# A decoder layer on one core: operand stacks filled from their half tiles, semaphores of each stage, and the order in which feed-forward weights are turned

## The chip, the cores and the metric

The kernel runs on one core of one Trainium2 chip. Its engines work side by side and wait for each other through semaphores: TensorE (PE; its weight loads are PEld), VectorE (DVE), ScalarE (ACT), GpSimd (POOL) and SyncE (SP), which here only issues DMAs. The metric is the device time of one launch in microseconds (us). Time before is the median of three runs.

## The reference

One layer of a transformer decoder on 8 sequences of 256 tokens, width 512, everything in float32 precision (the kernel reaches it by splitting each operand in a high and a low part in fp32r and multiplying high by high, high by low and low by high).

```python
x = x + self_attention(layernorm(x))       # 16 heads, decay states, gated
x = x + cross_attention(layernorm(x), ctx, mask)
x = x + feed_forward(layernorm(x))         # w1, w2, w3 first quantized to NF4 and back

# cross-attention, per sequence b: x[b] and ctx[b] are taken as [channel 256][t 512]
q = Wq @ x[b] + bq;  k = Wk @ ctx[b] + bk;  v = Wv @ ctx[b] + bv
dot = einsum('hdt,hds->hts', q, k) / 4     # 16 heads of 16
dot = mask_t * mask_s * dot - (1 - mask_t * mask_s) * 1e6
out = einsum('hts,hds->hdt', softmax(dot) * mask, v)

# feed-forward, d_ff = 1408
h = silu(x @ w1.T) * (x @ w2.T);  y = h @ w3.T
```

## The kernel before

The three parts are three stages of one program, one after the other. Each has a block of its own, in which every engine has its own list of instructions, and ends with `clear`, a further block in which GpSimd clears the stage's semaphores: all engines meet before and behind it. Memory (`big`, of which the tiles q_big in the trace are parts) is handed from one stage to the next.

**Self-attention** (0 to 1460 us in the trace) is not touched but for its end. There it also computes the query and key projection of cross-attention's sequence 0, in `xhi` and `xlo` (a_wqk_h and a_wqk_l in the trace), and SP prepares the first operand stacks Q0 and K0 from them.

**Cross-attention** goes over 8 sequences ("batches") b, each of 4 quads (4 heads), each quad of 4 steps q of four score tiles; G = 4 * (quad in the batch) + q runs from 0 to 15. For sequence b+1, `take_projection` (VectorE, `full`), `high` (ScalarE, `hi`) and `low` (GpSimd or VectorE, `lo`) make the halves of the projections while b's scores are computed; the buffer x_lo is also `full`. Three pairs of stacks Q[b % 3] and K[b % 3] hold the operands of a score product: for each half e of 8 heads, three segments of 16 partitions (high, high, low for Q; high, low, high for K), then rows of the mask, and in Q one row (53) with the row maxima. A segment is filled by `fill_part`, 256 KB. TensorE computes the scores of a quad twice, first over 53 partitions (x_pm, line 1720) for VectorE to find each row's maximum; the maxima are turned by TensorE (line 1725, one product for each quad), sent out to DRAM and back into row 53 (`rows`, two DMAs behind a wait), and then the product over 54 partitions (x_pd, line 1734) feeds the exponential on ScalarE. The products with V (x_pa, line 1748) follow.

SP's order in cross-attention is written out: at every step of G it waits for `dot_ready`, then issues what is due. The list `FILLS` says which segments of which stack go out at which G, `SECOND` says it for sequence 1. `put_part` (and `put` in self-attention) writes a half tile to DRAM (512 KB), and `fill_part` reads it back in the stack's layout; 4 puts and 12 fills for each sequence. `rows(t + 1)` stands at q = 1, `spread` at q = 0, `store` at q = 3 of every second quad.

**Feed-forward** first turns the three weights (22 + 11 tiles of 4 transposes each, TensorE line 2010, bf16) into `w1`, `w2`, `w3`, of which ScalarE and VectorE copy every second tile from a bank of pa; the loop `TILES` sets the order, w1, w2, w3. Then the first 512 tokens are turned, and `step` runs four times over 512 tokens: products with w1 and w2 (f_pa, f_pb, line 2028), silu, high and low, products with w3 (f_po, line 2042).

## Time and profile before

| | |
|---|---|
| median of 3 runs | 2402.73 us (2401.16 to 2409.71) |
| the profiled execution | 2406.03 us, span 2404.3 us |
| mean granted TensorE clock | 0.943 of full speed |
| PE busy | 2189.0 us (91%) |
| PEld, DVE | 1535.4 (64%), 1602.9 us (67%) |
| ACT, POOL | 791.9 (33%), 761.2 us (32%) |
| PE waits for x_K<-parts_scratch before x_pm | 23.9 us |

The profiled execution is one more run, its time 1.7 us longer than its span (from first to last instruction); it stands 3.3 us above the median. Busy shares are means over three stages with different limits. A row of a timeline or of a group names line, engine, operation and out<-in; what ended the idle time before an instruction stands in brackets behind it.

### The profile page before, as it was taken

Reading aid. Unit: us, or ns where it says so; the run is one execution under the profiler, and the core shown is the slowest. Engines: PE = TensorE matmul, PEld = TensorE weight load, DVE = VectorE, ACT = ScalarE, POOL = GpSimd, SP = SyncE. Lnnn points to the kernel's source line nnn. Section 1 sums busy time; section 2 is a strip of 40 time slices with the busy share of each in tenths; the row PEclk is TensorE's granted clock in tenths of the full one; section 3 lists DMA queues with packets and bytes.
Section 4 is the critical chain, followed back from the end, with each engine's and each line's share of the span. In section 5 each row is a group of like instructions: output and inputs, shape, how many; then the busy total and the mean of one; then the engine's idle time right before and its main releaser. Section 6 shows DMA issues by size and latency. Waiting matters only on the chain. (4 is left out here: it accounts for less than half of the span.)

```text
span 2404.3 us, 35495 instructions
## 1 busy us (share of the span) xinstructions
PE 2189.0 (91%) x11638; PEld 1535.4 (64%) x11638; DVE 1602.9 (67%) x2880; ACT 791.9 (33%) x1836; POOL 761.2 (32%) x532
## 2 busy tenths in 40 slices
PE   6899999999998999999999994988888887589998
PEld 4677778777776787778878772333332332167777
DVE  6668788788875568878878853687676876342221
ACT  1313323322332322332232320355444555432221
POOL 3334434533533433433443332112211220112122
PEclk9999999999999999999999996798898998669999
DMA  5211101101102201101110025765556643201100
GB/s 192 85 39 51 37 26 50 56 7 56 50 33 71 97 2 57 50 19 44 50 56 7 28 47 143 121 125 117 117 94 121 133 106 79 87 35 53 53 35 18
DMA packets 58838, 159.05 MB, mean 66 GB/s; under 512 B 9615, under 2 KB 24407, under 8 KB 52215
## 3 DMA queue, kind: packets, MB, share of 16 engines
q1 hardware_dynamic: 57142, 155.82, 24.9%
q10 hardware_dynamic: 1600, 2.02, 0.2%
q8 instruction: 52, 0.85, 0.2%
q14 instruction: 44, 0.35, 0.1%
HBM read 115.09 MB, written 34.33 MB: 62 GB/s over the span
## 5 line engine op out<-in xcount | busy, mean ns | idle before, releaser
L1627 DVE TENSOR_REDUCE x_mx<-x_pm 128x1 f32<-128x512 f32 x512 | 315.9, 679 | 108.4 <-PE x_pm L1720 107.2
L1490 ACT ACTIVATE x_E<-x_pd 128x512 f32<-128x512 f32 x512 | 265.4, 603 | 216.5 <-PE x_pd L1734 215.8
L1084 PE MATMUL a_pj<-q_big,a_wqk_h 128*128 128x512 f32 x1024 | 290.0, 405 | 1.0 <-POOL a_wqk_l L634 1.0
L1100 PE MATMUL a_pj<-a_wvg_h,q_big 128*128 128x512 f32 x1024 | 286.1, 406 | 1.1 <-DVE a_rm L790 1.0
L1100 PEld LDWEIGHTS a_pj<-a_wvg_h,q_big 128*128 128x128 f32 x1024 | 185.3, 188 | 51.8 <-DVE a_rm L790 2.4
L1084 PEld LDWEIGHTS a_pj<-q_big,a_wqk_h 128*128 128x128 f32 x1024 | 182.9, 188 | 40.4 <-POOL a_wqk_l L634 1.5
L790 DVE TENSOR_TENSOR a_rm<-a_pj,a_rope 128x1024 f32<-128x1024 f32 x128 | 155.7, 1217 | 79.4 <-PE a_pj L1084 78.1
L526 ACT ACTIVATE a_v<-a_pj 128x256 f32<-128x256 f32 x128 | 49.1, 384 | 416.0 <-PE a_pj L1100 416.0
L666 POOL TENSOR_TENSOR a_ogl<-a_ogf,a_ogh 128x512 fp32r<-128x512 f32 x64 | 81.7, 1298 | 286.6 <-ACT a_ogf L562 286.6
L1748 PE MATMUL x_pa<-x_E,x_vx 128*32 128x512 f32 x1024 | 149.8, 660 | 0.0
L862 DVE TENSOR_TENSOR a_acc<-a_po,a_acc 128x512 f32<-128x512 f32 x128 | 85.9, 687 | 93.7 <-PE a_po L1213 93.7
L1720 PE MATMUL x_pm<-x_K,x_Q 53*128 53x512 f32 x320 | 112.6, 484 | 32.1 <-DMA x_K<-parts_scratch 23.9
L1100 PE MATMUL a_pj<-a_wvg_l,q_big 128*128 128x512 f32 x512 | 140.7, 397 | 0.0
L1084 PE MATMUL a_pj<-q_big,a_wqk_l 128*128 128x512 f32 x512 | 140.1, 395 | 0.0
L1734 PE MATMUL x_pd<-x_Q,x_K 54*128 54x512 f32 x320 | 109.3, 494 | 21.5 <-ACT x_E L1490 17.3
L1734 PEld LDWEIGHTS x_pd<-x_Q,x_K 54*128 54x128 f32 x320 | 45.5, 196 | 127.8 <-ACT x_E L1490 72.2
L1857 POOL TENSOR_TENSOR f_hl<-f_hf,f_hh 128x512 fp32r<-128x512 f32 x44 | 56.6, 1285 | 213.2 <-ACT f_hh L1898 213.2
L796 DVE RECIPROCAL a_enz<-a_mid 128x512 f32<-128x512 f32 x32 | 107.2, 3351 | 16.7 <-PE a_mid L1068 16.7
L1100 PEld LDWEIGHTS a_pj<-a_wvg_l,q_big 128*128 128x128 f32 x512 | 96.7, 189 | 23.5
L553 ACT ACTIVATE a_sq<-a_po 128x128 bf16<-128x128 f32 x256 | 67.2, 277 | 133.9 <-PE a_po L1125 133.0
L1084 PEld LDWEIGHTS a_pj<-q_big,a_wqk_l 128*128 128x128 f32 x512 | 96.0, 187 | 23.4
L1213 PE MATMUL a_po<-a_wo_h,a_ogh 128*128 128x512 f32 x256 | 106.1, 414 | 3.0 <-POOL a_ogl L666 3.0
(215 smaller groups left out, 4573.5 us busy)
## 6 DMA issues: line engine op xcount, KB each, us to landing
a_qk_raw<-in_wqk SPq DMA_DIRECT2D x16, 1024.0 KB, 5.5
a_vg_raw<-in_wvg SPq DMA_DIRECT2D x16, 1024.0 KB, 4.9
q_big<-parts_scratch SPq DMA_DIRECT2D x36, 256.0 KB
...
```

What stands on the lines that cost most here:

```text
L666: nc.gpsimd.tensor_tensor(ogl[:, h, :], ogf[:, h, :], ogh[:, h, :].bitcast(F32), ALU.subtract).then_inc(ogl_done, 1)
L790: nc.vector.tensor_tensor(turned, pb, table, ALU.mult).then_inc(roped_m, 1)
L796: nc.vector.reciprocal(enz[:, p], ps[:, 0, :].rearrange("p (t m) -> p t m", t=4)).then_inc(enz_done, 1)
L862: nc.vector.tensor_tensor(a, po[:, tt % 2, :], a, ALU.add).then_inc(added, 1)
L1084: last = mm(pj[:, j % 2, :], wa[:, c, j * P:(j + 1) * P], xa[:, c, p * UT:(p + 1) * UT], start=k == 0, stop=k == 11)
L1100: last = mm(pj[:, tt % 2, :], xa[:, c, t0:t0 + P], wa[:, c, :], start=k == 0, stop=k == 11)
L1213: last = mm(po[:, tt % 2, :], oa[:, h, tt * P:(tt + 1) * P], wa[:, h, :], start=k == 0, stop=k == 5)
L1490: nc.scalar.activation(E[:, n % ESLOTS, :], pd[:, n % 3, :], ACT.Exp, scale=XD ** -0.5).then_inc(exp_done, 1)
L1627: nc.vector.reduce_max(mx[:, u % 2, at:at + 1], pm[:, k % 3, :], AX_X).then_inc(pm_done, 1)
L1720: mm(pm[:, k % 3, :], Q[b % 3][z, hp, q * P:(q + 1) * P], K[b % 3][z, hp, :], start=True, stop=True).then_inc(pm_ready, 1)
L1734: mm(pd[:, n % 3, :], K[b % 3][z, hp, q * P:(q + 1) * P], Q[b % 3][z, hp, :], start=True, stop=True).then_inc(dot_ready, 1)
L1748: last = mm(pa[32 * i:32 * i + 32, 0, :], vx[:, b % 3, q, head(t, i)].rearrange("p d k -> p (d k)"), E[:, k % ESLOTS, :], start=q == 0, st ...
```

## The change

Three things are changed together.

1. `fill_part` takes a segment of a stack straight from the half tiles in SBUF (64 partitions of 4 KB to 16 partitions of 16 KB). `put`, `put_part`, the DRAM tensor `parts` and their semaphores are gone. With them `FILLS` changes: in the second half of each batch all 12 fills for b+2 are issued (before: most in the first half of b+1). Since a fill now reads `hi` and `lo`, VectorE waits in `take_projection(b, 0)` for all fills of the stack b-1.
2. The semaphores of a stage come from a scope of their own, and are cleared by GpSimd inside the next stage: self-attention's behind `values(1, 1)` in cross-attention, cross-attention's behind `prepare(0)` in feed-forward. The two blocks between the stages are gone.
3. In feed-forward w1 and w2 are turned first, in pairs, w1 in pa and w2 in pb, the copies being divided anew (VectorE the first 7 tiles of w2, ScalarE the others), with the turns of x between the last pairs. The 11 tiles of w3 are turned inside the first `step`, one behind each pair of products, in the banks of po, and copied by ScalarE (`take_w3`). x comes in two halves, and `ident` on ScalarE's queue.

```diff
-def clear(nc, semaphores):
-
-    with nc.Block() as block:
-        @block.gpsimd
-        def _(pool):
-            for sem in semaphores:
-                pool.sem_clear(sem)
+def clear(pool, semaphores):
+
+    for sem in semaphores:
+        pool.sem_clear(sem)
...
-def fill_part(dma, tile, w, e, seg, split_dram, sem):
+def fill_part(dma, tile, w, e, seg, halves, sem):
 
     z = slice(64 * e + 16 * seg, 64 * e + 16 * seg + 16)
-    dma(tile[z].bitcast(F32),
-        split_dram[ORDERS[w][seg], w, 64 * e:64 * e + 64].rearrange("(r j) o t -> r (j o) t", j=4)).then_inc(sem, 16)
+    dma(tile[z].bitcast(F32), halves[ORDERS[w][seg]][64 * e:64 * e + 64, 2 * w:2 * w + 2].bitcast(F32)).then_inc(sem, 16)
...
+            fill(Q0, 0)
             store(1, 0)
-            put(1, ck_out)
-            sp.wait_ge(ck_out, 32)
-            for e in range(2):
-                for seg in range(3):
-                    fill_part(sp.dma_start, K0, 1, e, seg, split_dram, stack_0)
+            fill(K0, 1)
             store(1, 1)
             sp.wait_ge(stack_0, 16 * 16)
             sp.wait_ge(out_done, 16 * HALVES * HTILES)
...
-    clear(nc, s.used)
...
-        FILLS = [(0, (2,)), (0, (3,)), (0, (4, 5)), (1, (0, 1)), (1, (2,)), (1, (3,)), (1, (4, 5))] + 9 * [(0, ())]
+        FILLS = 8 * [(0, ())] + [(0, (0, 1)), (0, (2, 3)), (0, (4, 5)), (1, (0, 1)), (1, ()), (1, (4, 5)), (1, (2,)), (1, (3,))]
...
-            def put_part(b, w, part):
-                n = slice(2 * w, 2 * w + 2)
-                if b > 1 and not w and not part:
-                    sp.wait_ge(stack_in[(b - 1) % 3], stacked(b - 1))
-                sp.wait_ge((hi_done, lo_done)[part], 4 * (b - 1) + 2 * w + 2)
-                sp.dma_start(split_dram[part, w], (hi, lo)[part][:, n].bitcast(F32)).then_inc((q_split, k_split)[w], 16)
-
...
             def stack(b, w, pieces):
                 for k in pieces:
-                    if k == 0:
-                        sp.wait_ge((q_split, k_split)[w], 32 * b)
-                    fill_part(sp.dma_start, (Q, K)[w][b % 3], w, k % 2, k // 2, split_dram, stack_in[b % 3])
+                    part = ORDERS[w][k // 2]
+                    sp.wait_ge((hi_done, lo_done)[part], 4 * (b - 1) + 2 * w + 2)
+                    fill_part(sp.dma_start, (Q, K)[w][b % 3], w, k % 2, k // 2, (hi, lo), stack_in[b % 3])
 
...
             rows(0)
-            for w in range(2):
-                for part in range(2):
-                    put_part(1, w, part)
...
-                        stack(b + 1, *(FILLS if b else SECOND)[G])
+                    if not b:
+                        stack(1, *SECOND[G])
                     if t == 0 and q == 2:
                         load_c(2)
                     if b + 2 < B:
                         if G in (6, 7):
                             mask_rows(b + 2, G - 6)
-                        if 9 <= G < 13:
-                            put_part(b + 2, (G - 9) // 2, (G - 9) % 2)
+                        stack(b + 2, *FILLS[G])
                         if G == 12 and b + 3 < B:
                             load_x(b + 3)
                         if G == 13 and b + 3 < B:
                             load_c(b + 3)
-                        if G >= 14:
-                            stack(b + 2, 0, (G - 14,))
...
             values(1, 0)
             values(1, 1)
+            clear(pool, spent)
             for b in range(B):
...
-                    after(dve, (q_split, k_split)[j // 2], 32 * (b - 1))
+                    if j == 0 and b > 1:
+                        dve.wait_ge(stack_in[(b - 1) % 3], stacked(b - 1))
                     nc.vector.scalar_tensor_tensor(full[:, j, :], src[:, 0, :], bqk_t[:, j:j + 1], mb[:, b % 4],
...
-    clear(nc, s.used)
-
-
-def feed_forward(nc, x2_in, raw, big, ident_in, identb_in, out):
...
-        TILES = []
-        for i, w in enumerate((w1, w2)):
-            for r in range(FT):
-                TILES.append((i, [(slice(r * D + c * P, r * D + (c + 1) * P)) for c in range(C)],
-                              w[:, :, r * P:(r + 1) * P]))
-        for r in range(FT):
-            TILES.append((2, [slice(q * FF + r, q * FF + r + (P - 1) * FT + 1, FT) for q in range(4)],
-                          w3[:, r, :].rearrange("p (d q) -> p q d", q=4)))
+        BY_DVE = 7
+        MIXED = FT - 3
+
+        def turned(i, r):
+
+            return pa[:, r % 2, 0:256].bitcast(BF16) if i == 0 else pb[:, r % 2, 0:256].bitcast(BF16)
+
...
 
             prepare(0)
+            clear(pool, spent)
             step(0, True)
...
-            for t, (i, cols, dst) in enumerate(TILES):
-                if t % 2 == 0:
-                    act.wait_ge(w_ready, t + 1)
-                    src = pa[:, t % 2, 0:256].bitcast(BF16)
-                    nc.scalar.activation(dst, src.rearrange("p (q n) -> p q n", q=4), ACT.Copy).then_inc(taken_act, 1)
+            act.dma_start(ident[:], ident_in).then_inc(ident_done, 16)
+
+            def take(i, r):
+                act.wait_ge(w12_ready, 2 * r + i + 1)
+                nc.scalar.activation((w1, w2)[i][:, :, r * P:(r + 1) * P], spread(turned(i, r)), ACT.Copy).then_inc(taken_act, 1)
+
+            def take_w3(r):
+                act.wait_ge(w3_ready, r + 1)
+                nc.scalar.activation(w3[:, r, :].rearrange("p (d q) -> p q d", q=4), spread(po[:, r % 2, 0:256].bitcast(BF16)),
+                                     ACT.Copy).then_inc(w3_taken, 1)
 
...
+            def take(r):
+                dve.wait_ge(w12_ready, 2 * r + 2)
+                V.tensor_copy(w2[:, :, r * P:(r + 1) * P], spread(turned(1, r))).then_inc(taken_dve, 1)
+
+            for r in range(BY_DVE - 2):
+                take(r)
             norm_stats(0)
+            for r in range(BY_DVE - 2, BY_DVE):
+                take(r)
             normed(0, 0)
             normed(0, 1)
-            for t, (i, cols, dst) in enumerate(TILES):
-                if t % 2 == 1:
-                    dve.wait_ge(w_ready, t + 1)
-                    src = pa[:, t % 2, 0:256].bitcast(BF16)
-                    V.tensor_copy(dst, src.rearrange("p (q n) -> p q n", q=4)).then_inc(taken_dve, 1)
-            for pair in range(2):
-                if pair:
-                    normed(0, 2)
-                    normed(0, 3)
-                for tt in (2 * pair, 2 * pair + 1):
-                    low(0, tt)
+            low(0, 0)
+            normed(0, 2)
+            low(0, 1)
+            normed(0, 3)
+            low(0, 2)
+            low(0, 3)
...
-                after(pe, taken[t % 2], t // 2)
-                for q, col in enumerate(cols):
-                    last = nc.tensor.transpose(pa[:, t % 2, q * 64:(q + 1) * 64].bitcast(BF16), raw[:, i, col], identb[:])
-                last.then_inc(w_ready, 1)
-            for tt in range(4):
...
+            def turn(i, r):
+                if r >= 2 and i and r - 2 < BY_DVE:
+                    pe.wait_ge(taken_dve, r - 1)
+                elif r >= 2:
+                    pe.wait_ge(taken_act, by_act(i, r - 2))
+                for c in range(C):
...
+            def turn_w3(r):
+                if r >= 2:
+                    pe.wait_ge(w3_taken, r - 1)
+                for q in range(4):
+                    last = nc.tensor.transpose(po[:, r % 2, q * 64:(q + 1) * 64].bitcast(BF16),
+                                               raw[:, 2, q * FF + r:q * FF + r + (P - 1) * FT + 1:FT], identb[:])
+                last.then_inc(w3_ready, 1)
+
+            for r in range(FT):
+                turn(0, r)
+                turn(1, r)
+                if r == MIXED:
+                    pe.wait_ge(ident_done, 16)
+                if r >= MIXED:
+                    transpose_x(0, r - MIXED)
+            transpose_x(0, 3)
+            pe.wait_ge(taken_act, 2 * FT - BY_DVE)
+            pe.wait_ge(taken_dve, BY_DVE)
...
                         last.then_inc(ready, 1)
+                    if isinstance(g, int) and g == 0:
+                        turn_w3(f)
+                if isinstance(g, int) and g == 0:
+                    pe.wait_ge(w3_taken, FT)
...
-    clear(nc, s.used)
+    with nc.Block() as block:
+        @block.gpsimd
+        def _(pool):
+            clear(pool, signals.used)
```

How instructions move, at three places. First SyncE's queue at the end of self-attention, where the halves of sequence 0's projections (a_wqk_h and a_wqk_l) become the first stacks. Before:

```order
L463 DMA parts_scratch<-a_wqk_h 128x1024 [waits a_chi_done]
L463 DMA parts_scratch<-a_wqk_l 128x1024 [waits a_clo_done]
L126 DMA q_big<-rows_scratch 5x8x512 [waits a_vg_ready]
L126 DMA q_big<-rows_scratch 5x8x512
L126 DMA q_big<-rows_scratch 6x8x512 x2
L133 DMA q_big<-parts_scratch 16x4096 [waits a_cq_out]
L133 DMA q_big<-parts_scratch 16x4096 x5
L368 DMA x_scratch<-a_acc 128x512 [waits a_added] x4
L463 DMA parts_scratch<-a_wqk_h 128x1024 [waits a_chi_done]
L463 DMA parts_scratch<-a_wqk_l 128x1024 [waits a_clo_done]
L133 DMA q_big<-parts_scratch 16x4096 [waits a_ck_out]
L133 DMA q_big<-parts_scratch 16x4096 x5
```

Now:

```order
L123 DMA q_big<-rows_scratch 5x8x512 [waits sa_vg_ready]
L123 DMA q_big<-rows_scratch 5x8x512
L123 DMA q_big<-rows_scratch 6x8x512 x2
L130 DMA q_big<-a_wqk_h 16x4x1024 [waits sa_chi_done]
L130 DMA q_big<-a_wqk_h 16x4x1024
L130 DMA q_big<-a_wqk_h 16x4x1024 [waits sa_chi_done]
L130 DMA q_big<-a_wqk_h 16x4x1024
L130 DMA q_big<-a_wqk_l 16x4x1024 [waits sa_clo_done]
L130 DMA q_big<-a_wqk_l 16x4x1024
```

The two transfers to DRAM are gone, and each fill waits for the half tile itself. (The K0 stack's fills follow in the same manner behind x_scratch<-a_acc.)

Second, SyncE's queue in the second half of a batch of cross-attention, from a `spread` (x_att<-x_raw) to the next. Before:

```order
L1428 DMA x_att<-x_raw 64x512 [waits x_x2_done,x_raw_done,x_dot_ready]
L1429 DMA x_sums<-x_raw 64x512
L1417 DMA maxima_scratch<-x_mT 16x128 [waits x_row_b,x_pm_done,x_dot_ready]
L1420 DMA x_Q<-maxima_scratch 1x1024 [waits x_max_out]
L1420 DMA x_Q<-maxima_scratch 1x1024
L1399 DMA parts_scratch<-x_hi 128x1024 [waits x_hi_done,x_stack_0]
L1399 DMA parts_scratch<-x_lo 128x1024 [waits x_lo_done,x_dot_ready]
L1436 DMA x_scratch<-x_xt 128x512 [waits x_x2_done,x_dot_ready]
L1399 DMA parts_scratch<-x_hi 128x1024 [waits x_hi_done]
L1428 DMA x_att<-x_raw 64x512 [waits x_x2_done,x_raw_done,x_dot_ready]
L1429 DMA x_sums<-x_raw 64x512
```

Now:

```order
L1409 DMA x_att<-x_raw 64x512 [waits sx_x2_done,sx_raw_done,sx_dot_ready]
L1410 DMA x_sums<-x_raw 64x512
L130 DMA x_Q<-x_hi 16x4x1024 [waits sx_hi_done] x2
L1398 DMA maxima_scratch<-x_mT 16x128 [waits sx_row_b,sx_pm_done,sx_dot_ready]
L1401 DMA x_Q<-maxima_scratch 1x1024 [waits sx_max_out]
L1401 DMA x_Q<-maxima_scratch 1x1024
L130 DMA x_Q<-x_hi 16x4x1024 [waits sx_hi_done] x2
L130 DMA x_Q<-x_lo 16x4x1024 [waits sx_lo_done,sx_dot_ready]
L130 DMA x_Q<-x_lo 16x4x1024 [waits sx_lo_done]
L1417 DMA x_scratch<-x_xt 128x512 [waits sx_x2_done,sx_dot_ready]
L130 DMA x_K<-x_hi 16x4x1024 [waits sx_hi_done] x2
```

Each put of 512 KB has given its place to two to four fills of 256 KB, which now stand between the same `rows`, `store` and `spread`.

Third, TensorE at the start of feed-forward. Before, all transposes of weights, then those of x, then the first products:

```order
L2010 MATMUL f_pa<-f_identb,w_raw 128x128 x132
L2004 MATMUL f_pt<-f_ident,f_xn 128x128 x16
L2028 MATMUL f_pa<-q_big,f_w 128x512 x4
L2028 MATMUL f_pa<-f_xl,f_w 128x512 x4
L2028 MATMUL f_pb<-q_big,f_w 128x512 x4
```

Now, the last three pairs of w1's and w2's tiles and what follows:

```order
L2015 MATMUL f_pa<-f_identb,w_raw 128x128 x4
L2015 MATMUL f_pb<-f_identb,w_raw 128x128 x4
L2006 MATMUL f_pt<-f_ident,f_xn 128x128 x4
L2015 MATMUL f_pa<-f_identb,w_raw 128x128 x4
L2015 MATMUL f_pb<-f_identb,w_raw 128x128 x4
L2006 MATMUL f_pt<-f_ident,f_xn 128x128 x4
L2015 MATMUL f_pa<-f_identb,w_raw 128x128 x4
L2015 MATMUL f_pb<-f_identb,w_raw 128x128 x4
L2006 MATMUL f_pt<-f_ident,f_xn 128x128 x8
L2048 MATMUL f_pa<-q_big,f_w 128x512 x4
L2048 MATMUL f_pa<-f_xl,f_w 128x512 x4
L2048 MATMUL f_pb<-q_big,f_w 128x512 x4
```

The x transposes (f_pt) have moved in between the last tiles of the weights, and w3's 44 transposes have moved behind the first products, four after each f.

## Rows read from the trace of the kernel before

**Rows 1.** Windows: start:end, length; PE, PEld, DVE, ACT, POOL busy; clock, DMA share, GB/s.

```profile
0.00:1420.00 1420.00, 1370.39 (x7931) 1090.57 (x7932) 1078.47 (x1993) 413.94 (x1114) 563.31 (x355) 0.99 0.15 49
...
1460.00:1464.00 4.00, 0.00 (x0) 0.00 (x0) 0.00 (x0) 0.00 (x0) 0.00 (x0) 0.81 1.10 131
...
1632.00:1640.00 8.00, 6.86 (x18) 2.49 (x18) 3.24 (x5) 1.08 (x2) 0.00 (x0) 0.50 0.31 41
```

**Rows 2.** Timeline, end of self-attention: start, busy us, line, form, [idle before].

```profile
1459.07 0.69 DVE L862 TENSOR_TENSOR a_acc<-a_po,a_acc 128x512 f32<-128x512 f32 x1 [0.71 <-PE a_po L1213]
...
1479.59 0.10 POOL L1517 MEMSET x_half_neg<- 128x2 f32 x1 [28.54 <-POOLq L107]
```

**Rows 3.** Waits of SP's queue, 1400 to 2100: sum, times, longest, us.

```profile
SPq L133 <- DMA parts_scratch<-a_wqk_l: 19.6, 2, 18.1
...
SPq L107 <- PEq L107: 10.6, 2, 7.4
```

**Rows 4.** DMA issues: queue, count, KB each, median us to landing.

```profile
x_att<-x_raw SPq DMA_DIRECT2D x32, 128.0 KB, 2.9
```

**Rows 5.** Waits of TensorE, 1520 to 2080: sum, times, longest, us.

```profile
PE x_pm L1720 <- DMA x_K<-parts_scratch: 23.9, 5, 6.3
...
PE x_pm L1720 <- DMA q_big<-parts_scratch: 7.9, 2, 4.5
...
PE x_pd L1734 <- DMA q_big<-maxima_scratch: 4.5, 2, 3.8
```

**Rows 6.** Timeline, TensorE, two batches of cross-attention.

```profile
1608.60 0.33 PE L1725 MATMUL x_pm<-x_ident,x_mx 128*128 128x128 f32 x1
...
1627.62 0.33 PE L1725 MATMUL x_pm<-x_ident,x_mx 128*128 128x128 f32 x1
...
1633.14 0.80 PE L1720 MATMUL x_pm<-x_K,x_Q 53*128 53x512 f32 x2 [5.18 <-DMA x_K<-parts_scratch]
...
1654.12 0.33 PE L1725 MATMUL x_pm<-x_ident,x_mx 128*128 128x128 f32 x1
...
1973.77 0.33 PE L1725 MATMUL x_pm<-x_ident,x_mx 128*128 128x128 f32 x1
...
2014.64 0.33 PE L1725 MATMUL x_pm<-x_ident,x_mx 128*128 128x128 f32 x1
...
2027.36 0.33 PE L1725 MATMUL x_pm<-x_ident,x_mx 128*128 128x128 f32 x1
```

**Rows 7.** Timeline, VectorE, SP and TensorE, first batch, quads 1 and 2.

```profile
1551.56 0.75 DVE L1613 SCALAR_TENSOR_TENSOR x_lo<-x_pp,x_bqk,x_mb 128x512 f32<-128x512 f32 x1 [2.60 <-PE x_pp L1704]
...
1557.39 0.77 SPq L133 DMA_DIRECT2D x_K<-parts_scratch  x2
...
1563.98 0.50 PE L1720 MATMUL x_pm<-x_K,x_Q 53*128 53x512 f32 x2 [1.06 <-DMA x_K<-parts_scratch]
```

**Rows 8.** Timeline, start of feed-forward and its first product.

```profile
2093.57 0.10 POOL L1846 MEMSET f_half_neg<- 128x4 f32 x1 [9.89 <-POOLq L107]
...
2095.78 1.03 PE L2010 MATMUL f_pa<-f_identb,w_raw 128*128 128x128 bf16 x8 [16.83 <-DMA f_ident<-in_ident]
...
2135.84 1.62 PE L2028 MATMUL f_pa<-q_big,f_w 128*128 128x512 f32 x3 [1.50 <-DVE f_xl L1939]
```

**Rows 9.** Groups by form, 2093 to 2136: busy, mean ns, idle before.

```profile
L2010 PE MATMUL f_pa<-f_identb,w_raw 128*128 128x128 bf16 x132 | 18.4, 311 | 31.5 <-DMA f_ident<-in_ident 16.8 <-DVE f_w L1980 12.0 <-DVE q_big L1980 1.4
...
L1980 DVE CAST f_w<-f_pa 128x512 fp32r<-128x512 bf16 x11 | 7.6, 691 | 7.0 <-PE f_pa L2010 7.0
...
L1877 ACT ACTIVATE f_w<-f_pa 128x512 fp32r<-128x512 bf16 x11 | 6.6, 597 | 32.8 <-PE f_pa L2010 32.8
```

**Rows 10.** Chain that ended last: start us, us, what.

```profile
2127.00 1.10 ACT q_big L1877
...
2135.84 3.75 PE f_pa L2028 x8
...
2142.47 1.81 PE f_pa L2028 x8
```

97 lines of the change are left out of this document (54 added, 43 removed).

## The prediction

> **What bounds the kernel now.** I read the mean clock and the 40 slices first, then windows by stage, then the chain of waits, TensorE's waits and the timelines at the seams. Self-attention is TensorE's: it is busy 1370 of its first 1420 us [rows 1], and the change does not touch that part. The rest has three kinds of gap. At the seam behind self-attention the last addition ends at 1459.76 (1459.07 + 0.69) and cross-attention's first instruction comes at 1479.59: 19.8 us in which no engine computes [rows 2]. In cross-attention TensorE waits 23.9 us in 5 waits for fills of K, 7.9 in 2 for fills of the stack in `big`, and 4.5 in 2 for row maxima [rows 5]. Before feed-forward's first product lie 42.3 us (2093.57 to 2135.84) in which TensorE is busy 18.4 us with turning weights [rows 8, 9]. The change aims at all three, so I price them one by one, against the profiled execution's own 2406.0 us, which stands 3.3 us above the median of 2402.7.
>
> **Seam self to cross: -16.5 us.** SP waited 18.1 us in one piece for a half tile's landing in DRAM before it could issue K0's fills [rows 3], so these ran behind the end of the arithmetic: DMA share 1.10 at 131 GB/s after 1460, in a stretch in which every engine is idle [rows 1]. By that rate a fill of 256 KB takes 2.0 us of the queues' whole capacity, six take 12 us, and the stage's last store stood behind them. Then GpSimd cleared 98 semaphores while the others waited 7.4 us (75 ns each) [rows 3]. Now each fill waits only for its half tile, so the fills should be through before the last addition; what remains is the last store, priced by the nearest transfer, x_att<-x_raw, 2.9 us [rows 4], and 0.4 us to leave the block: 3.3 instead of 19.8. The clearing now stands on GpSimd after `values(1, 1)`, where it has some us of nothing to do before it divides for the first pairs; hidden, and if not, 7.4 us on GpSimd, which TensorE would only notice through `lo`. Bounds: -9 (the fills still late by half) to -17.
>
> **Cross-attention, the waits: -46 us.** A wait costs more than its length, since the clock falls after it: after the wait of 5.18 us at 1633.14 the stretch to 1640 has clock 0.50, which is 1.2 GHz, where self-attention had 0.99 (2.4 GHz) [rows 1, 6]. So I compare whole quads by the one product that turns the maxima. In batch 1 the quad from 1608.60 took 19.0 us and the next, which holds the wait, 26.5 us; it has some eight products more, for which I take 1 us, so the wait of 5.18 cost about 6.5. Batches 2 to 5 have one such wait each, between 3.4 and 5.9 us, and read in the same way lose 6.3, 6.8, 6.9 and 3.9 us: with batch 1 30.4. In batch 6 two quads took 40.9 us (1973.77 to 2014.64), the next one of the same content 12.7 us: 15.5 us lost, to the longest wait for K (6.3 us) and the longest for maxima (3.8 us) [rows 5, 6]. Sum 45.9. Now all twelve fills for b+2 are issued in G 8 to 15 of b, a whole batch (73.0 us: (1973.77 - 1608.60) / 5) before they are read, so these waits should go. Bounds: -25 to -50. It goes by a half if maxima rows queue behind the fills (rival B).
>
> **A new wait in batch 0: +11 us.** VectorE now waits in `take_projection(b, 0)`, at G 5, for all fills of the stack b-1, because `full` lies over `lo`. For b = 2 this is the stack of sequence 1, whose fills go by `SECOND` up to G 5 itself. In the trace VectorE is at that instruction at 1551.56, the last K fills of that list are issued from 1557.39 on, and the product behind them comes at 1563.98 [rows 7]. Without the puts ahead of them I put the landing 3 us earlier, near 1560: VectorE stands 8.4 us, and behind it stand all row maxima, so TensorE stands as well. The old wait there (1.06 us) goes. 7.3 us times 1.5, since here too the clock falls: 11. Bounds: 7 (no clock loss) to 15 (the landing where it was). For b > 2 the fills are through by G 15 or shortly after, five steps before; that wait costs nothing.
>
> **DMA in the second half of a batch: 0.** Twelve fills of 2.0 us are 24 us of transfer in some 37 us (half of 73), where before four puts and two fills stood, 512 and 256 KB. `rows`, `spread` and `store` share SP's queue with them. Every issue of SP also takes time: the pair of fills at 1557.39 took 0.77 us [rows 7]; four more such pairs are 3 us of issuing, spread over eight steps. I take nothing, and rival B for the rest. The price of a fill from SBUF instead of DRAM is not in the trace. Nearest is x_att<-x_raw, SBUF to SBUF, 128 KB in 2.9 us to the landing [rows 4], which speaks for no more than 2 us of transfer. The Trainium skill ("SBUF — State Buffer", section on the DMA port swizzle) lets 16 adjacent partitions reach four of sixteen ports, about 109 GB/s together, which by estimate is 2.4 us for a fill. The row of 131 GB/s, measured on fills into 16 partitions each, several at once, stands above it, and the sum goes by the row; by the page's figure twelve fills would take 29 us and still fit.
>
> **Seam cross to feed-forward: -3.2 us.** Both clearings cost SP 10.6 us together, 7.4 at most [rows 3]; the second's 3.2 us go, as cross-attention's semaphores are cleared behind `prepare(0)` on GpSimd, which then waits for ScalarE's first `high` anyway. The last store stays on the path.
>
> **Feed-forward: -16.9 us.** A tile of four transposes cost TensorE 0.56 us (18.4 / 33), a copy 0.69 on VectorE and 0.60 on ScalarE [rows 9]. Before, 33 tiles went in turn, with a stop for VectorE's statistics of x. Now: 2.2 us until the first transpose, as before [rows 8]; 7 pairs of w1, w2 by VectorE and ScalarE at 1.1 us (TensorE's two tiles) are 7.7; the last 4 pairs are ScalarE's, 1.2 for two copies, and three of them carry a `high` of 1.10 [rows 10]: 8.1; then the last x turn, `high` and `low`: 2.7. Sum 20.7, where it was 42.3: -21.6. Back come the 11 tiles of w3 in the first step: 0.28 us each if the transposes halve at full clock, 0.56 if not; I take 0.35, +3.9. The wait for the last copy of w3 is one copy, +0.7. Their banks are po's, free until the first product with w3; their copies (1.1 us by the nearest, `high`) fit in ScalarE's slack between products of 1.81. Net -17.0, bounds -13 to -21: the first pair of products took 3.75 at the low clock against 1.81 at the high one [rows 10], and if the denser turning has raised the clock by then, 3 us more are won.
>
> **Sum.** -16.5 - 46 + 11 - 3.2 - 17.0 = -71.7: 2334.3 by the profiled execution, 2331 by the median.
>
> **Rivals.** B: maxima rows come late. At G 9 `rows` is issued behind the fills of G 8, at G 1 behind those of G 14 and 15: two fills of 2.0 us are 4 us in each of six batches, 24 us, if nothing hides them. For it: TensorE already waited for maxima in two places, 4.5 us [rows 5]. Against it: the row is issued at q = 1 and read at the next quad's start. It gives 2355.
> D: more is won. The batch 0 stall ends earlier because the fills' wait on `lo` is the only one left, the middle gives its upper bound and the clock is up by feed-forward's products: 2331 - 8 - 5 - 3 = 2315.
> C, the other side: a fill from SBUF is slower, since 64 partitions of 4 KB pieces are read where DRAM gave long runs. At 4 us for a fill the twelve take 48 us; with the 11 us of other transfers in 37 us of time 22 us stay over in each of six batches (132), batch 0's list costs 30 more, the seam 14: +176, or 2507. It outweighs the gain from about 2.8 us for a fill on (72 / 88 us for each us above 2.0). The 2.9 us of x_att<-x_raw speak against it. The same page of the Trainium skill gives 64 source partitions eight ports, so by it the source would not be the narrow side; no row here shows that.
> E: fills at about 2.7 us: the middle and the seam give back what is won, 2395 to 2408.
>
> **How the numbers follow.** Forecast 0.60 (2318 to 2342), B 0.18, D 0.13, C 0.04, E 0.05. The range reaches over D and B and leaves out C, E and tails: 2306 to 2360. Within 0.5% (12 us, about what a measurement of this kernel can tell from no change): most of E, 0.04. Faster 0.92, slower 0.04.
>
> **What would show it.** Seam: POOL's first instruction of cross-attention 3 to 4 us behind the last addition. Middle: no wait of TensorE for x_K fills from batch 1 on, third quads of 19 to 20 us, clock 0.99. Batch 0: VectorE idle some 8 us before the first `full`, released by a DMA into x_K. Feed-forward: first product 21 us after its start, four short transposes behind each f in the first step. The prediction is wrong if fills take more than 2.5 us each, or if waits for maxima rows of over 1 us stand at most quads.

## The result and the profile after

The changed kernel took 2380.84 us (median of 4 runs, 2361.68 to 2391.24) against 2404.76 of the kernel before (4 runs beside them). The ratio is 0.989 (95% interval 0.984 to 0.993): 1.1% faster, clear of the noise but small, where 3.0% were forecast, and outside the forecast range of 2306 to 2360. A second set of four runs (below) gave 0.984 (0.979 to 0.989). The profiled execution took 2374.18 us, 31.9 less than that of before, where the sum had -71.7.

The page of the changed kernel has almost the same shares as that of before: TensorE's busy time has even grown by 8.6 us for the same 11,638 matmuls. In cross-attention, from the first turn of maxima to the last, it grew from 476 to 490 us, at a mean clock of 0.86 where the kernel before had 0.89.

```profile
PE 2197.6 (93%) x11638; PEld 1535.0 (65%) x11638; DVE 1595.7 (67%) x2871; ACT 799.3 (34%) x1845; POOL 761.9 (32%) x532
...
PEclk9999999999999999999999997687888998789999
```

Cut by the steps of the prediction, each piece taken between the same two instructions in both traces (us; the 15.1 us from cross-attention's first instruction to its first turn of maxima are alike in both):

| piece | before | after | difference | forecast |
|---|---|---|---|---|
| last addition to first instruction of cross-attention | 19.8 | 2.5 | -17.3 | -16.5 |
| first turn of maxima to the fifth (batch 0) | 87.5 | 104.3 | +16.8 | +11 |
| fifth to the last (batches 1 to 7) | 470.3 | 461.5 | -8.8 | -46 |
| last turn to feed-forward's first instruction | 41.0 | 41.8 | +0.8 | -3.2 |
| feed-forward's first instruction to the end | 310.7 | 288.0 | -22.7 | -17.0 |

The seam, in the timelines of VectorE and GpSimd [rows 2]:

```profile
1458.43 0.69 DVE L851 TENSOR_TENSOR a_acc<-a_po,a_acc 128x512 f32<-128x512 f32 x1 [0.71 <-PE a_po L1202]
...
1461.62 0.10 POOL L1491 MEMSET x_half_neg<- 128x2 f32 x1 [11.05 <-POOLq L184]
```

The addition ends at 1459.12, and GpSimd starts 2.5 us later. Batch 0, in the timelines of TensorE, SyncE, VectorE and TensorE again [rows 7]:

```profile
1491.62 3.11 PE L1680 MATMUL x_pp<-x_cx,x_wk 128*128 128x512 f32 x4 [4.14 <-DMA x_cx<-in_ctx]
...
1542.92 1.19 SPq L130 DMA_DIRECT2D x_K<-x_hi  x2
...
1549.59 0.75 DVE L1589 SCALAR_TENSOR_TENSOR x_lo<-x_pp,x_bqk,x_mb 128x512 f32<-128x512 f32 x1 [12.46 <-DMA x_K<-x_hi]
...
1551.00 0.79 PE L1696 MATMUL x_pm<-q_big 53*128 53x512 f32 x1 [8.37 <-DVE x_mx L1603]
```

The foreseen wait is there: VectorE stands 12.46 us for K's last fills, issued at 1542.92 and landed at 1549.5, TensorE 8.37 behind it. The other row was not foreseen: 4.14 us for x_cx.

In batches 1 to 6 no wait for a fill is left [rows 5], as forecast. In its place, in TensorE's waits from 1570 on (sum, times, longest):

```profile
PE x_pd L1710 <- DMA x_Q<-maxima_scratch: 18.6, 4, 4.9
...
PE x_pd L1710 <- DMA q_big<-maxima_scratch: 9.1, 2, 5.4
```

27.7 us in six waits of 3.8 to 5.4 us, one in each batch, for row 53 of the stack, 4.6 on the mean. SyncE's queue shows how one of them comes about (batch 1 at G 11 to 13), and then TensorE:

```profile
1660.02 0.37 SPq L1417 DMA_DIRECT2D x_scratch<-x_xt  x1
...
1660.43 1.19 SPq L130 DMA_DIRECT2D q_big<-x_hi  x2
...
1662.05 0.51 SPq L1409 DMA_DIRECT2D x_att<-x_raw  x1
...
1665.95 0.39 SPq L1368 DMA_DIRECT2D x_xt<-x_scratch  x1
...
1666.96 0.36 SPq L1398 DMA_DIRECT2D maxima_scratch<-x_mT  x1
...
1673.72 0.53 SPq L1401 DMA_DIRECT2D x_Q<-maxima_scratch  x2
```

```profile
1675.52 0.79 PE L1710 MATMUL x_pd<-x_Q,x_K 54*128 54x512 f32 x2 [4.86 <-DMA x_Q<-maxima_scratch]
```

The step G 12 begins with the `spread` at 1662.05. Two fills were issued just before it. SyncE waits for a store to land before it may load x (1665.95), and only then sends out the maxima, at 1666.96. They are in DRAM, and SyncE can fetch them back, at 1673.7, 6.8 us later (in the kernel before it took 4.0, and they were sent 3.2 us behind the `spread` and not 4.9). The two transfers into row 53 land at 1675.5, when TensorE has stood for 4.86 us.

Feed-forward, in the timelines of GpSimd and TensorE [rows 8]:

```profile
2084.37 0.10 POOL L1826 MEMSET f_half_neg<- 128x4 f32 x1 [6.67 <-POOLq L1294]
...
2102.33 1.20 PE L2048 MATMUL f_pa<-q_big,f_w 128*128 128x512 f32 x4 [1.50 <-DVE f_xl L1938]
...
2107.68 0.45 PE L2022 MATMUL f_po<-f_identb,w_raw 128*128 128x128 bf16 x4
```

The first product comes 18.0 us behind the stage's start (before 42.3, forecast 20.7), and a turn of w3 is 0.45 us long behind each f, or 0.38 from one f to the next.

### The profile page after: what moved, and what is told of

The parts are those of the page before. It is cut to its first block and busy times, and to the rows that moved or that the text cites. A ratio compares the mean times of both kernels' runs of the same rounds, so it can differ in the third digit from the quotient of the medians.

```text
span 2372.4 us, 35407 instructions
## 1 busy us (share of the span) xinstructions
PE 2197.6 (93%) x11638; PEld 1535.0 (65%) x11638; DVE 1595.7 (67%) x2871; ACT 799.3 (34%) x1845; POOL 761.9 (32%) x532
## 5 line engine op out<-in xcount | busy, mean ns | idle before, releaser
L1724 PE MATMUL x_pa<-x_E,x_vx 128*32 128x512 f32 x1024 | 160.5, 705 | 0.0
L1710 PE MATMUL x_pd<-x_Q,x_K 54*128 54x512 f32 x320 | 116.9, 535 | 33.7 <-DMA x_Q<-maxima_scratch 18.6
L785 DVE RECIPROCAL a_enz<-a_mid 128x512 f32<-128x512 f32 x32 | 107.3, 3352 | 16.8 <-PE a_mid L1057 16.8
L1089 PEld LDWEIGHTS a_pj<-a_wvg_l,q_big 128*128 128x128 f32 x512 | 96.2, 188 | 23.2
L1959 DVE TENSOR_TENSOR f_hf<-f_pb,f_sil 128x512 f32<-128x512 f32 x44 | 30.4, 691 | 118.9 <-PE f_pb L2048 118.9
```

The costliest lines, as they stand in the source:

```text
L785: nc.vector.reciprocal(enz[:, p], ps[:, 0, :].rearrange("p (t m) -> p t m", t=4)).then_inc(enz_done, 1)
L1089: last = mm(pj[:, tt % 2, :], xa[:, c, t0:t0 + P], wa[:, c, :], start=k == 0, stop=k == 11)
L1710: mm(pd[:, n % 3, :], K[b % 3][z, hp, q * P:(q + 1) * P], Q[b % 3][z, hp, :], start=True, stop=True).then_inc(dot_ready, 1)
L1724: last = mm(pa[32 * i:32 * i + 32, 0, :], vx[:, b % 3, q, head(t, i)].rearrange("p d k -> p (d k)"), E[:, k % ESLOTS, :], start=q == 0, st ...
```

## The experiments

Turns of maxima are used as a clock throughout: one stands at each quad, so the distances between them are the lengths of quads. A batch is measured from the turn of quad 0 of batch 2 to that of batch 6 (four batches): before 73.6 us, after 71.7. "Median" is over 4 to 10 runs, with the ratio to the kernel before in the same set of runs and its 95% interval; kernels of different sets compare by this ratio. In the lists below Q01 stands for pieces 0 and 1 of the next Q stack, K4 for piece 4 of K, and - for a step without a fill. Piece k is segment k // 2 of half k % 2.

| kernel | median | ratio | a batch |
|---|---|---|---|
| gap | 2382.3 | 0.991 (0.989 to 0.992) | 75.1 |
| second | 2365.4 | 0.984 (0.983 to 0.986) | 75.2 |
| mask | 2371.7 (one run) | | 76.7 |
| even | 2348.9 | 0.974 (0.969 to 0.979) | 71.7 |
| even_early | 2328.6 | 0.968 (0.962 to 0.975) | 70.9 |
| even2 | 2332.6 | 0.970 (0.966 to 0.975) | 71.9 |
| even3 | 2306.2 | 0.959 (0.956 to 0.962) | 64.8 |
| actq | 2423.9 | 1.005 (1.003 to 1.008) | 83.6 |
| own_blocks | 2383.9 | 0.990 (0.986 to 0.994) | 73.3 |
| ffn | 2384.7 | 0.990 (0.985 to 0.994) | 73.6 |
| over_dram | 2402.0 | 0.999 (0.997 to 1.001) | 72.5 |
| over_dram2 | 2390.7 | 0.995 (0.993 to 0.998) | 71.1 |
| after_again | 2361.4 | 0.984 (0.979 to 0.989) | 71.6 |

**bench**, transfers by themselves, each group behind a wait for the one ahead:

```python
for w, tile in enumerate((Q, K)):       # a burst, from SBUF or from DRAM
    for k in range(6):
        kind(sp.dma_start, tile, w, k, many)
sp.dma_start(maxima[0], mT[:].bitcast(F32)).then_inc(put, 16)   # the path of a row
sp.wait_ge(put, n)
```

> A kernel that computes nothing of the layer: it times transfers on an otherwise idle core, and writes x out as it came. One at a time: four puts of 512 KB, four fills from SBUF, four from DRAM; then bursts of twelve fills from SBUF, from DRAM, and both again; then the path of a maxima row (8 KB out, then two of 4 KB back) alone and behind 2, 4 and 6 fills of K of either kind on the same queue, and behind 6 fills issued on ScalarE's queue. The prediction took 2.0 us for a fill of either kind, 24 to 25 us for a burst of twelve. If fills from SBUF are the slower kind, their burst takes over 30 us. If the row only shares the DMA engines with the fills, its path is as late behind fills on another queue as on its own; if it stands in line behind them, the path grows by about 2 us for each fill on its own queue alone.

SyncE's timeline (a line without a wait inside it is one go, x the number of transfers):

```profile
28.84 13.68 SPq L130 DMA_DIRECT2D b_Q<-b_hi  x4
...
46.32 12.31 SPq L2101 DMA_DIRECT2D b_Q<-parts_scratch  x4
...
62.35 2.65 SPq L130 DMA_DIRECT2D b_Q<-b_hi  x4
...
91.34 2.62 SPq L2101 DMA_DIRECT2D b_Q<-parts_scratch  x6
...
119.86 2.67 SPq L130 DMA_DIRECT2D b_Q<-b_hi  x4
...
176.36 0.30 SPq L2143 DMA_DIRECT2D maxima_scratch<-b_mT  x1
...
177.70 0.52 SPq L2147 DMA_DIRECT2D b_Q<-maxima_scratch  x2
...
208.12 0.59 SPq L2143 DMA_DIRECT2D maxima_scratch<-b_mT  x1
...
219.50 0.52 SPq L2147 DMA_DIRECT2D b_Q<-maxima_scratch  x2
...
261.79 0.30 SPq L2143 DMA_DIRECT2D maxima_scratch<-b_mT  x1
...
267.91 0.52 SPq L2147 DMA_DIRECT2D b_Q<-maxima_scratch  x2
...
279.00 0.30 SPq L2143 DMA_DIRECT2D maxima_scratch<-b_mT  x1
...
288.64 0.52 SPq L2147 DMA_DIRECT2D b_Q<-maxima_scratch  x2
```

Four fills alone, from SBUF, take 28.84 to 46.32, 4.4 us each to the landing; from DRAM 46.32 to 62.35, 4.0. A burst of twelve from SBUF takes 29.0 us (62.35 to 91.34), from DRAM 28.5 (to 119.86), and a second pair of bursts 28.9 and 27.6. So both kinds cost 2.4 us for a fill in a burst, 3.1 MB at 108 GB/s: the fill from SBUF isn't slower (rival C is out), but neither is worth the 2.0 us that the prediction took. The Trainium skill's figure ("SBUF — State Buffer", the DMA port swizzle), 2.4 us by estimate, agrees with the runs. A row's way out takes 1.3 us alone (176.36 to 177.70) and 11.4 us behind six fills (208.12 to 219.50); with the six on ScalarE's queue it took 6.1 us (261.79 to 267.91). With six fills from DRAM it took 12.3 us behind them and 9.6 with them on ScalarE's queue (279.00 to 288.64).

**gap** leaves G 10 to 12 free:

```diff
-FILLS = 8*[-] + [Q01, Q23, Q45, K01, -, K45, K2, K3]
+FILLS = 8*[-] + [Q01, Q23, -, -, -, Q45, K01, K45];  LATE = [-, K23] + 14*[-]
```

> Edit to the changed kernel: FILLS leaves G 10 to 12 free. Q's last two segments go out behind the maxima row at G 13, K's at G 14, 15 and (two of them) at G 1 of the next batch. Theory 1: the new waits of TensorE for maxima rows (six of 3.8 to 5.4 us, each once in a batch, at the quad after G 13) come from the row's two transfers standing behind the six to eight fills and loads issued just before; then they fall under 1 us, the batch shortens from 71.5 us to about 65, and the whole becomes about 33 us shorter than the changed kernel (2345). Theory 2: a fill from SBUF takes more of the queues' time than 2.0 us in all, so the row is late wherever it stands; then the waits only move (to the row of G 1) and the time stays within 8 us of the changed kernel.

The waits for maxima are gone, and there are six others, longer: 4.5 to 8.3 us, 41.6 in all. In the timelines of SyncE, VectorE and TensorE, batch 2 at its first quad:

```profile
1674.74 0.53 SPq L1399 DMA_DIRECT2D maxima_scratch<-x_mT  x1
...
1686.38 0.52 SPq L1402 DMA_DIRECT2D x_Q<-maxima_scratch  x2
...
1686.30 0.95 DVE L1618 RECIPROCAL x_sums<-x_sums 128x128 f32<-128x128 f32 x1 [6.79 <-DMA x_sums<-x_raw]
...
1687.85 0.79 PE L1699 MATMUL x_pm<-x_K,x_Q 53*128 53x512 f32 x1 [6.97 <-DVE x_mx L1606]
```

VectorE waits for the sums that it is to invert, since their transfer stands behind the six fills of G 13 to 15; TensorE waits 6.97 us for VectorE. A batch of 75.1 us. Theory 1's cause (small transfers behind fills) holds for the row of G 13, its forecast of 2345 does not: what was cleared at one place was piled up at another, which is what theory 2 said of the time.

**second** issues the fills of sequence 1 ahead of the loop, **mask** only holds the mask rows back, and with them the load of x that is issued behind them:

```diff
+            for w in range(2):
+                stack(1, w, range(6))        # second; SECOND in the loop goes
+            sp.wait_ge(lo_done, 4)           # mask
             mask_rows(1, 0)
             mask_rows(1, 1)
```

> Edit to the changed kernel: the twelve fills for sequence 1 are issued ahead of SyncE's loop, behind the first maxima row and before the mask rows, where the transfers to DRAM stood before the change, instead of in pairs at G 0 to 5. Theory 1: VectorE's wait of 12.5 us in batch 0 at its first half tile (and TensorE's of 8.4 us behind it) falls to nothing, and so does TensorE's wait of 4.1 us for x_cx, since the mask rows no longer run beside that load; batches 0 and 1 get 18 to 22 us shorter. Theory 2: the fills only crowd out the maxima rows of batch 0, whose waits take the place of this one; then batch 0 gets no more than 5 us shorter.

> Edit to the changed kernel: SyncE waits for the last low half tile of sequence 1 before it issues the mask rows of stack 1, as it did before the change through the transfers to DRAM that stood ahead of them. Theory 1: the load of x_cx, 11.3 us to its landing, is slow because the mask rows (5 and 6 partitions of 16 KB) now run beside it; with the wait it takes 4 to 5 us again, TensorE's wait of 4.1 us for x_cx goes, and the first quad (from the first turn of maxima to the second) takes 28 to 30 us instead of 34.6. Theory 2: the load is slow for another reason (the constants' loads); then the 34.6 us stay.

In both the wait for x_cx is gone and the first quad takes 28.6 and 28.5 us instead of 34.6: what ran beside that load was its cause. That can be the mask rows or the load of x (512 and 256 KB) behind them, for every run that moved the one moved the other. In second VectorE's wait in batch 0 is gone too (that quad 22.6 us instead of 33.7), and a part of it is back as a row behind twelve fills (SyncE, then TensorE):

```profile
1509.15 0.32 SPq L1398 DMA_DIRECT2D maxima_scratch<-x_mT  x1
...
1530.15 0.54 SPq L1401 DMA_DIRECT2D q_big<-maxima_scratch  x2
...
1531.99 0.80 PE L1710 MATMUL x_pd<-q_big 54*128 54x512 f32 x2 [8.93 <-DMA q_big<-maxima_scratch]
```

From the first turn to the fifth, second is 8.2 us shorter than the changed kernel, and to the first turn of batch 2 13.4 (6.9 against after_again), less than the 18 to 22 of theory 1, since 8.9 us of wait in batch 0 are back at the row. The ratio of second, 0.984, is not clear of the changed kernel's 0.984 to 0.989.

**even** issues one fill for each step, **even_early** adds a mended start:

```diff
+FILLS = 8*[-] + [Q0, Q1, Q2, Q3, Q4, Q5, K0, K1];  LATE = [K4, K5, K2, K3] + 12*[-]     # even
+            stack(1, 0, range(6))            # even_early, ahead of the loop
+            stack(1, 1, (0, 1))              # the other four at G 1, mask rows at G 2
```

> Edit to the changed kernel: one fill for each step, at G 8 to 15 and G 0 to 3 of the next batch, instead of the twelve in G 8 to 15. The timing kernel gave 2.4 us for each fill in a burst and a maxima row that is 2 us later for each fill ahead of it. Theory 1 (small transfers stand in line behind fills): with one fill in 3.2 us nothing piles up, each row is late by at most one or two fills, 2 to 5 us, within its slack of some 9 us; no wait of TensorE over 1 us from batch 1 on, batches of about 64 us instead of 71.5, the whole 2335 to 2350. Theory 2 (the fills themselves take too much of the queues, wherever they stand): waits of 3 us and more appear at some other row, and the whole stays within 8 us of the changed kernel (2381).

> Both seen cures together: one fill for each step as in the kernel before this one in the list, and for sequence 1 eight fills ahead of the loop, the other four at G 1 behind the row, and the mask rows at G 2. Theory 1: VectorE's wait in batch 0 (12.5 us) and TensorE's for x_cx (4.1 us) go as well, 15 to 22 us less than the even kernel: 2315 to 2332. Theory 2 (the eight fills only make the row of G 1 late): TensorE waits 5 us or more at that row and the gain over the even kernel is under 10 us.

Both times came out within their theory 1: 2348.9 and 2328.6. The rest of theory 1 of even did not: it wanted no wait over 1 us and batches of 64 us. One wait of 1.5 to 1.8 us is left in each of batches 2 to 5 (TensorE in even):

```profile
1804.94 0.55 PE L1713 MATMUL x_pd<-x_Q,x_K 54*128 54x512 f32 x2 [1.84 <-DMA x_Q<-maxima_scratch]
```

With them these four batches take 71.7 us each, as long as in the changed kernel with its waits of 4.6 to 5.4: even gains in the batches that have no wait left, batch 1 (66.2 us, where the changed kernel has 77.2 in one trace and 70.8 in the other) and batch 6 (52.4 and not 59.6). Even_early has one wait of 1.6 to 2.0 us in each of batches 2 to 5 too, and one of 2.3 us in batch 1.

Both with the start of even_early, **even2** moves the load of x behind the row at G 13 and leaves G 12 free; **even3** also moves the load of ctx to G 4 and keeps G 0 free:

```diff
+FILLS = 8*[-] + [Q0, Q1, Q2, Q3, -, Q4, Q5, K0]
+LATE = [K1, K45, K2, K3] + 12*[-]        # even2, load_x at G 13, load_c at G 14
+LATE = [-, K14, K5, K23] + 12*[-]        # even3, load_c at G 4
```

> Edit to the even_early kernel: G 12 issues no fill, and the load of x (512 and 256 KB) moves from G 12 to behind the maxima row at G 13, that of ctx to G 14, so that before that row only the sums' transfers stand. In even_early TensorE still waited 1.6 to 2.0 us for this row in four batches, and behind each wait the clock was at 0.50 to 0.60 of full speed for a quad (17 to 19 us instead of 13.4). If the line in SyncE's queue is the cause, these waits go and with them 4 us of low clock for each: 2305 to 2318. If the wait comes from the row's own path (out, landing, back), it stays and the time stays within 6 us of even_early (2329).

> Edit to even2, in which VectorE waited 1.7 to 3.3 us in five batches for the sums' transfer, behind a fill and the load of ctx: the load of ctx moves from G 14 to G 4 of the batch that uses it, and K's first fills leave G 0 free. If the low clock behind each small wait is what keeps the kernels at 2329 to 2333, the batches 2 to 5 without any wait over 1 us take 63 to 66 us at clock 0.99 instead of 70 to 73, and the whole is 2300 to 2318. If the clock falls in these quads without a wait before it (TensorE's share of work there), batches stay at 70 us and the time at 2325 or more.

Even2 was no faster than even_early: the wait for the row had gone, and one for the sums had come in five batches, of 1.7 to 3.3 us:

```profile
1664.00 0.49 PE L1701 MATMUL x_pm<-x_K,x_Q 53*128 53x512 f32 x1 [2.03 <-DVE x_mx L1608]
```

Even3 has none of them. TensorE's waits from 1570 to 2000, and the window 1700 to 1800:

```profile
PE x_pd L1715 <- ACT x_E L1469: 25.5, 87, 0.8
...
PE x_pm L1701 <- DVE x_mx L1608: 12.0, 29, 0.9
...
PE x_pd L1715 <- DMA q_big<-maxima_scratch: 0.3, 1, 0.3
...
1700.00:1800.00 100.00, 89.60 (x455) 33.65 (x454) 85.03 (x146) 57.76 (x113) 21.63 (x20) 1.00 0.64 111
```

Not one wait of a microsecond, clock 1.00 over these 100 us, batches of 64.8 us, 2306.2 us in all. The clock is not full everywhere: by quads it is 1.00 in 25 of the 27 from batch 1 on, and 0.92 in the third quads of batches 1 and 5, which take 21.8 and 21.7 us although no wait of TensorE in them reaches 1 us. VectorE waits there, 2.0 and 1.9 us, for the last late fills of K to land before its first half tile. The window of the one in batch 1:

```profile
1590.51:1612.29 21.78, 19.49 (x80) 6.58 (x78) 15.28 (x25) 9.78 (x19) 2.54 (x2) 0.92 0.65 106
```

By the ratios to the kernel before (0.959, and 0.984 to 0.989) it is 2.5 to 3% faster than the changed kernel, and the fastest tried.

**actq**, the fills on ScalarE's queue, at their old steps:

```diff
-                        stack(b + 2, *FILLS[G])
+                    for k in pieces:                       # in ScalarE's loop, same G
+                        act.wait_ge((hi_done, lo_done)[...], ...)
+                        fill_part(act.dma_start, ...)
```

> Edit to the changed kernel: the fills keep their steps (G 8 to 15) but are issued by ScalarE on its own queue. If rows are late because they stand in line behind the fills in one queue, their waits shrink (the timing kernel: a row's way out took 6.1 us instead of 11.4 beside six fills) and TensorE's waits for maxima fall from 4.7 to under 2 us; if they are late because the fills take the DMA engines, the waits stay at 4 us or more. ScalarE pays 0.6 us for each issue and may itself become late at G 8 to 15 (its exponentials of a step take 2.4 of 3.2 us), which would show as waits of TensorE for x_E. I expect 2355 to 2375.

It came to 2423.9 us where 2355 to 2375 were expected, 0.5% slower than the kernel before. TensorE, then SyncE in the same batch:

```profile
1669.80 0.80 PE L1714 MATMUL x_pd<-x_Q,x_K 54*128 54x512 f32 x2 [4.32 <-DMA x_Q<-maxima_scratch]
...
1693.52 0.80 PE L1714 MATMUL x_pd<-x_Q,x_K 54*128 54x512 f32 x2 [4.60 <-DMA x_Q<-maxima_scratch]
...
1654.03 1.19 SPq L1398 DMA_DIRECT2D maxima_scratch<-x_mT  x1
...
1663.13 0.53 SPq L1401 DMA_DIRECT2D x_Q<-maxima_scratch  x2
```

The row sent out at 1654.03 was back 9.1 us later although no fill stood ahead of it in SyncE's queue, and the row of G 13 in the next quad after 11.1; in the changed kernel the same two rows took 5.4 (1648.01 to 1653.39) and 6.8 us. So a line in SyncE's own queue is not needed to make a row late: fills on another queue delay it as well. There is a second reason: on SyncE's queue the fills of G 9 go out only when the row is back in SyncE's hands, 1654.26 behind 1653.39, while ScalarE issued them at 1654.57 and 1655.17, right behind the row. How much each has of it was not measured. The row of 6.1 us in bench, sent when two of the six fills had been issued, had made the other queue look better than it is here. The Trainium skill ("DMA: Bandwidth & Descriptors", issuing engines are not separate DMA queues) has it that transfers run on the same 16 engines, whoever starts them; these rows agree with it.

**over_dram** and **over_dram2** are the kernel before with other lists, the fills over DRAM; over_dram2 also moves the loads of x and ctx as even3 does:

```diff
-FILLS = [Q2, Q3, Q45, K01, K2, K3, K45] + 9*[-];  Q0, Q1 at G 14, 15
+FILLS = [Q45, K01, K4, K5, K2, K3] + 10*[-];      Q0 to Q3 at G 12 to 15     # over_dram
+FILLS = [-, Q34, Q5, K01, K45, K23] + 10*[-];     Q0 to Q2 at G 13 to 15     # over_dram2
```

> The kernel before, fills still over DRAM, with only the list of fills moved: those for b+2 one at a time at G 12 to 15, the others at G 0 to 5 instead of G 0 to 6, so that the last is issued earlier. It asks how much of the gain of cross-attention comes from the times at which fills are issued and not from where they read. If the waits of TensorE for K fills (5.2 to 6.3 us, once in a batch) came from the list alone, they fall by 3 to 6 us and the kernel is 20 to 35 us faster than before (2370 to 2385). If the queues are too full with puts and fills together (8 x 0.25 + 12 x 0.25 MB for a batch), maxima rows are late in exchange and it stays within 12 us of before.

> The kernel before with the fills still over DRAM, issued at G 13 to 15 and G 1 to 5, and the loads of x and ctx moved as in even3 (x behind the row at G 13, ctx to G 4). over_dram had waits for maxima rows of 2.9 to 5.0 us in six batches, as the changed kernel has. If the times of issue decide and not what a fill reads, the waits fall to 2 us or less, batches take 64 to 68 us and the kernel, whose seams and feed-forward are as before, comes to 2360 to 2378. If the puts (four of 512 KB for a batch) are too much for the queues, waits of 3 us and more stay and it is over 2388.

Neither gave what was hoped for (2370 to 2385, 2360 to 2378). TensorE in over_dram and in over_dram2:

```profile
1668.48 0.80 PE L1734 MATMUL x_pd<-x_Q,x_K 54*128 54x512 f32 x2 [3.52 <-DMA x_Q<-maxima_scratch]
...
1703.60 0.50 PE L1720 MATMUL x_pm<-q_big 53*128 53x512 f32 x2 [3.77 <-DMA q_big<-parts_scratch]
```

Over_dram has the changed kernel's pattern, a wait for maxima of 2.1 to 5.0 us in each batch and one of 2.4 us for K. Over_dram2 has no more waits for maxima until batch 6, but waits for fills of 1.5 to 4.1 us and for x_cx. In these lists the fills start at G 12 or 13, behind the puts, and not at G 8, and some row, load or fill is late in each of them. By that, what reading from SBUF buys in cross-attention is four or five steps of lead, and the changed list spent them on being through by G 15 instead of on distance between the fills. That no list over DRAM could do better is not shown: two were tried.

**own_blocks** is the changed kernel with its clearings in blocks between the stages, **ffn** the kernel before with feed-forward changed alone:

> The changed kernel with its clearings back in blocks of their own between the stages. By the prediction's terms the clearing of self-attention's semaphores is worth 7.4 us of the seam's 17.3 and the other 3.2 us: 10 us longer than the changed kernel, 2391, with the first instruction of cross-attention 9 to 10 us behind the last addition instead of 2.5. If the clearing on GpSimd in the middle of batch 0 costs something there (late low halves), the first quads get shorter again and less than 8 us are lost.

> The kernel before with the changed feed-forward stage alone (with its semaphores cleared in a block of its own, as before). The changed kernel's trace has 288.0 us from the stage's first instruction to the end where the kernel before has 310.7, so 22 us less than before are expected: 2382, ratio 0.991. If it gives under 12 us, what shortened the stage was the state of the clock that the end of cross-attention left behind and not the new order.

The seam of own_blocks:

```profile
1460.57 0.69 DVE L854 TENSOR_TENSOR a_acc<-a_po,a_acc 128x512 f32<-128x512 f32 x1 [0.71 <-PE a_po L1205]
...
1471.12 0.10 POOL L1494 MEMSET x_half_neg<- 128x2 f32 x1 [18.61 <-POOLq L107]
```

1461.26 to 1471.12 is 9.9 us, where the changed kernel has 2.5 and the kernel before 19.8: the direct fills are worth 9.9 and the moved clearing 7.4. By the medians of the same set own_blocks lost 22 us on the changed kernel, not 10; 11 of it are seen in its trace at the two seams (GpSimd's idle time at the second is 10.7 us instead of 6.7), the other 11 lie within the spread of both kernels (20 us). Ffn has 287.5 us from the start of its last stage to the end, 23.2 less than before, and is 26 us faster: the new order does it by itself.

**after_again**, for the spread:

> The changed kernel again, beside the others on one chip, since its four runs spread from 2361.7 to 2391.2. Expected 2365 to 2392, and in its trace again six waits of TensorE for maxima rows of 3.5 to 5.5 us. What should differ from run to run is how long the clock stays at 0.5 behind each wait: quads behind it of either 16 and 19 us or 19 and 22 to 23 us.

2358.8 to 2379.0, with the same six waits (3.6 to 5.1 us); the median of 2361.4 lies below the 2365 expected. How much one wait can cost differs. Here are two windows of the changed kernel, the two quads of batch 4 right behind a wait of 4.7 us,

```profile
1819.00:1836.00 17.00, 16.51 (x67) 6.03 (x67) 12.62 (x25) 8.97 (x17) 0.71 (x1) 0.67 0.75 126
...
1836.00:1855.00 19.00, 17.62 (x79) 6.40 (x77) 15.32 (x25) 9.78 (x19) 2.55 (x2) 1.00 0.16 34
```

and in those of the same two quads in second, behind a wait of 4.8 us:

```profile
1813.00:1832.00 19.00, 19.00 (x67) 6.65 (x67) 13.65 (x26) 9.00 (x17) 0.71 (x1) 0.50 0.67 111
...
1832.00:1855.00 23.00, 22.58 (x80) 7.99 (x77) 14.88 (x24) 10.00 (x19) 2.54 (x2) 0.72 0.12 28
```

(the clock is the third figure from the end). In the one the clock comes back within the first quad, which takes 16.2 us, and the second takes 19.0; in the other it stays at 0.50, which is 1.2 GHz, through the whole of the first, 19.0 us, and into the second, 22.8. The changed kernel's own trace has both: 19.0 and 22.3 us behind the wait of batch 1, 16.2 and 19.0 behind those of batches 2 to 5.

## Why the prediction was wrong

**The step that failed is "DMA in the second half of a batch: 0"**, and with it "Cross-attention, the waits: -46". The 46 us were there: the K waits did go (in batch 1 the quad that held one fell from 26.5 to 18.5 us, 8.0 where I had counted 6.5), and from the fifth turn to the last even3 takes 413.9 us, 56 less than the kernel before. But a row of maxima came late in exchange in each of batches 1 to 6, 4.6 us of wait and, in most of them, 2 to 3 of low clock behind it, so four fifths of the forecast were given back. I had weighed the fills against the half batch as a sum (24 of 37 us) and not asked what stands at G 13 when eight fills, a store, the sums and 0.75 MB of loads have been issued in five steps. The signs that were to show it wrong missed this too: fills took 2.4 us and not over 2.5, and the waits stood at one quad in four and not at most.

**A fill of 2.0 us** came from the share and rate of a stretch at the seam [rows 1] in which stores ran as well; in a burst by itself it is 2.4. That brought twelve fills from 24 to 29 us, which alone would still have fitted. The sum was right to name the Trainium skill's figure beside the row and wrong to prefer the row.

**Rival B** was the right mechanism (its chance 0.18) at the wrong place: I put it at G 1 and G 9 with 4 us in each of six batches, and it stood at G 13 with 4.6 us and the clock behind it; 2355 was still too low.

**The price of a wait: 1.5 times its length** holds for some waits only. Three quads in batch 4 without a wait take 45.8 us (even3), with one of 4.7 us 53.0 (the changed kernel) or 59.6 (second, 4.8 us), and with one of 1.84 us 56.0 (even). That is 7 to 14 us for a wait of 4.7, or 1.5 to 3 times its length, and 10 for one of 1.8, over five times. The price does not go by the length.

**Batch 0: +11** measured +16.8, of which +11.9 are the foreseen wait (33.7 against 21.9 us for that quad; 12.5 on VectorE against 8.4) and +6.1 the quad in which the mask rows and the load of x crowd the load of ctx, since the puts that had held them back were gone. That was a second effect of the removed work that I had not looked for; mask shows it, for the two together.

**Seam: -16.5** measured -17.3, its two terms confirmed by own_blocks (9.9 and 7.4). **Seam cross to feed-forward: -3.2**: GpSimd's idle time fell by 3.2 as said, and the low clock in the last quad covered it: 0.63 of full speed over its 26 us where the kernel before had 0.78, and in after_again, at 1.00, the same piece takes 33.1 us and not 41.8. **Feed-forward: -17.0** measured -22.7: the start 18.0 us and not 20.7, the turns of w3 0.38 us each and not 0.35, the clock up from the second f on as the bound said.

**What stays open**: why the clock comes back in one run behind the same wait and in another only two quads later. No run here controls it. That its return differs is shown, and also that in even3, without waits of over 1 us, it is 1.00 in all but two quads from batch 1 on, and 0.92 in these two, beside VectorE's waits for fills; what lowered it there is open. Open is also what the spread from run to run comes from. The changed kernel has 20 to 30 us of it and even3 11, but gap and second, with waits of the same length or longer, have only 9 and 6.
